# Second norm, transposes and router products of tiles 0 to 11 moved into the attention stage's last octet, with both stages in one block

## The chip, the cores and the metric

The kernel runs on one core of a Trainium2 chip. The metric is the device time of one execution in microseconds (us); lower is better. The engines are TensorE (PE, with its weight loads as PEld), VectorE (DVE), ScalarE (ACT), GpSimd (POOL) and SyncE (SP, which here only starts DMAs). Each engine runs its own instructions in their written order and waits on semaphores for the others.

## The reference, cut to what matters

Tokens are 2048 rows of 512 numbers (32 batches of 64). Two residual blocks are computed in float32:

```python
x = x + tanh(g_xattn) * xattn(layernorm(x), ctx, Wq, Wk, Wv, Wo)     # 32 heads of 128, 4 key/value heads
x = x + tanh(g_ffn)   * ffn(layernorm(x), router, experts, shared)
# ffn, for xt = layernorm(x):
scores = softmax(xt @ router_w + router_b) + router_bias             # 16 experts, 4 groups
# keep the best 2 groups, of these the best 2 experts; gate = their scores
y = sum over experts e of gate[:, e] * ((silu(xt @ w1 + b1) * (xt @ w2 + b2)) @ w3 + b3)
z = (silu(xt @ sw1 + sb1) * (xt @ sw2 + sb2)) @ sw3 + sb3            # shared expert, 256 wide
return y + z
```

## The kernel before, in words

The residual `y` stays on the chip as 16 tiles of 128 tokens by 512. Every float32 operand of a product is split into a rounded high part and the rest (`x_hi`, `x_lo`), and a product is three matmuls (`three_pass`, lines 84 to 86).

**Three stages, each in a block of its own.** Stage one makes keys, values and the transposed tokens. Stage two (`stage_two`) is attention: 128 steps m = 0 to 127, one for each of 4 key/value heads and 32 batches, grouped in octets of 8 steps; `octet(15, 3, NKV)` is the last octet, steps 120 to 127, and three more steps (128 to 130) let the pipeline run out. In step m PE computes the scores of batch m (L832, L834), turns the probabilities of batch m-1 (L872), projects queries for a later quad (only up to step 123), weighs the values of batch m-1 (`weigh`, into `ps_o`) and does half of an output projection (12 matmuls into `ps_y`). ACT copies the cross part of the scores (L672), makes `p_hi` (L678), the exponentials (L683) and `o_hi` (L691). DVE folds the scores (L758), takes the maximum (L760), makes `p_lo` (L763), adds an output pair to `y` (L738) or takes its statistics (L744), scales the probabilities (L779, `p_sb`) and makes `o_lo` (L783). In steps 120 to 127 DVE also aggregates one mean and variance a step (L749), and after step 130 the last eight together.

**Stage three** (`stage_three`) begins when all engines have left stage two. SP loads seven small tensors and the first half of the shared expert's weights; ACT loads the table for the square root and makes `std` of all 16 tiles; DVE takes the reciprocal. Then a front over 16 tiles: DVE normalises the even tiles and POOL the odd ones into a ring of 8 (`normed`); SP stores each to `xn_table`; PE transposes it into one of two banks (L1816); ACT makes `x_hi` (L1454) and DVE `x_lo` (L1585). After four tiles each, PE computes router products (`octet_logits`, L1793 and L1795, 8 matmuls), ACT copies them, and PE turns them (L1804). In between lie the splits of the shared weights and of `b3`. When the logits of all 16 tiles are turned, DVE starts the routing (L1625 and what follows): softmax, top-2, ranks, one-hot matrices (L1691 to L1696), slot tables (L1703 to L1709), while PE runs the shared expert's up products (`pe_up`, 24 matmuls an octet of tokens). Then come 31 slots of 256 rows each (gather, expert, scatter) and the end, which adds the experts' outputs and the second half of the shared expert to `y`.

Of the kernel before, what the change touches and what calls it, by code (L numbers as in the profile page):

```python
# [27 lines left out]
P = 128  # L28
# [64 lines left out]
def stage_one(nc, a, common, scratch):  # L93
# [4 lines left out]
    common["mean_var3"] = kept.enter_context(nc.sbuf_tensor("mean_var3", [P, TILES, 2], F32))  # L98
    scratch["k_full"] = nc.dram_tensor("k_full", (NKV, QUADS, P, QB * KEYS), F32, kind="Internal").ap()
    scratch["v_full"] = nc.dram_tensor("v_full", (NKV, QUADS, KEYS, QB, DH), F32, kind="Internal").ap()  # L100
    common["handed"] = handed = ExitStack()
    h = Buffers(nc, handed)
    w_raw = [h.sb(f"w_raw{i}", [P, 1024]) for i in range(2)]
    with ExitStack() as before:
# [3 lines left out]
    common.update(w_raw=w_raw, xt0=xt0, wq0=wq0, raw_in=[h.sem(f"raw_in{i}") for i in range(2)],  # L108
                  xt_in=[h.sem(f"xt_in{i}") for i in range(2)], w_hi_made=h.sem("w_hi_made"),
                  w_lo_made=h.sem("w_lo_made"))  # L110
# [369 lines left out]

def stage_two(nc, a, common, scratch):
    y, ident, gain = common["y"], common["ident"], common["gain_attn"]
    with ExitStack() as stack:  # L483
# [7 lines left out]
        kt = [b.sb(f"kt{i}", [P, 2, QB, KEYS], F32R) for i in range(2)]  # L491
        vt = [b.sb(f"vt{i}", [KEYS, QB, 2, DH], F32R) for i in range(2)]
        kt_raw = b.sb("kt_raw", [P, QB, KEYS])
        vt_raw = b.sb("vt_raw", [KEYS, QB, DH])
        q_hi = [b.sb(f"q_hi{i}", [P, QB, HG, SQ], F32R) for i in range(2)]
        q_lo = [b.sb(f"q_lo{i}", [P, QB, HG, SQ], F32R) for i in range(2)]
# [17 lines left out]
        kt_in = b.sem("kt_in")  # L514
        vt_in = b.sem("vt_in")
        k_hi_made = b.sem("k_hi_made")
        k_lo_made = b.sem("k_lo_made")
        v_hi_made = b.sem("v_hi_made")
        v_lo_made = b.sem("v_lo_made")
        stats_made = b.sem("stats3_made")  # L520
        w_hi_made, w_lo_made = common["w_hi_made"], common["w_lo_made"]
        queries = b.sem("queries")
        q_hi_made = b.sem("q_hi_made")
        q_lo_made = b.sem("q_lo_made")
        scored = b.sem("scored")
        cross_copied = b.sem("cross_copied")
        folded = b.sem("folded")
        max_made = b.sem("max_made")
        exp_made = b.sem("exp_made")
        rsums_made = b.sem("rsums_made")  # L530
        p_made = b.sem("p_made")
        p_turned = b.sem("p_turned")
        p_hi_made = b.sem("p_hi_made")
        p_lo_made = b.sem("p_lo_made")
        weighted = b.sem("weighted")
        o_hi_made = b.sem("o_hi_made")
        o_lo_made = b.sem("o_lo_made")
        halves = b.sem("halves")
        added = b.sem("added")
# [28 lines left out]
        block = stack.enter_context(nc.Block())  # L568

        @block.sync  # L570
        def _(sp):
# [59 lines left out]
        @block.scalar  # L631
        def _(act):
# [32 lines left out]
            def step(s, o, g):  # L665
# [32 lines left out]
                for i in splits_at(s.t, o, j):  # L698
                    split_piece(g, i)

# [10 lines left out]
        @block.vector  # L711
        def _(dve):
# [33 lines left out]
            def aggregate(tile):  # L746

                dve.wait_ge(stats_made, STEPS // 2 - TILES + tile + 1)
                dve.bn_aggr(mean_var[:, tile, :], stats[:, tile, :])  # L749

            def step(s, o, g):
# [19 lines left out]
                if isinstance(s.t, int) and s.t == STEPS // 8 - 1:  # L771
                    aggregate(j)
# [18 lines left out]
                for i in splits_at(s.t, o, j):  # L791
                    split_piece(g, i)

# [11 lines left out]
            for tile in range(8, TILES):  # L805
                aggregate(tile)

        @block.tensor
        def _(pe):
# [65 lines left out]
            def step(s, o, g):  # L875
# [7 lines left out]
                if s.query:  # L883
                    if p == 0:

                        pe.wait_ge(xt_in[quad_parity], 16 * (t + 1 + j // 4))
                    if last_octet and j >= 4:

                        pe.wait_ge(w_lo_made, PIECES * g + p + 1)

                    pe.wait_ge(q_lo_made, 4 * s.quad + p - 1)
                    project_queries(s.quad, quad_parity, p, 0)
                    project_queries(s.quad, quad_parity, p, 1)
                if s.pv:
                    weigh(s)
# [12 lines left out]
            for j in range(3):  # L908
                step(Step(16, j), 0, NKV)
    common["handed"].close()  # L910
# [12 lines left out]
class SharedHalf:  # L923
# [3 lines left out]
    def __init__(self, b, half, work, weights, ps_up, ps_down, y, moe):  # L927
# [7 lines left out]
        self.gate_copied = b.sem(f"s_gate_copied{half}")  # L935
# [18 lines left out]
    def act_silu(self, act, o):  # L954
# [3 lines left out]
        if o >= 2:  # L958
            act.wait_ge(self.h_made, o - 1)
        act.activation(self.silu[r][:], self.ps_up[2 * r][:], ACT.Silu,  # L960
                       bias=self.moe["shared_bias"][:, 0, self.half:self.half + 1]).then_inc(self.silu_made, 1)

    def act_gate(self, act, o):
        r = o % 2

        act.activation(self.h_sb[r][:], self.ps_up[2 * r + 1][:], ACT.Identity,
# [54 lines left out]
    def pe_up(self, pe, o, copied=False):  # L1021
# [10 lines left out]
        tokens = slice(512 * o, 512 * o + 512)  # L1032
        for k in range(2):
            for c in range(C):
                n = slice(INTER * c, INTER * c + INTER)
                last = three_pass(pe, self.ps_up[2 * r + k][:], self.w_hi[:, k, n], self.w_lo[:, k, n],
                                  self.moe["x_hi"][:, c, tokens], self.moe["x_lo"][:, c, tokens],
                                  c == 0, c == C - 1)
        last.then_inc(self.up_done, 1)
# [21 lines left out]
def stage_three(nc, a, common, scratch, out):  # L1061
# [7 lines left out]
    mean_var = common["mean_var3"]  # L1069
# [3 lines left out]
    RING = 8  # L1073
    CONSTS = 22
    WARM = 14
    with ExitStack() as stack:
        b = Buffers(nc, stack)
        x_hi = b.sb("x_hi", [P, C, T], F32R)
        x_lo = b.sb("x_lo", [P, C, T], F32R)
# [4 lines left out]
            "shared_bias": b.sb("shared_bias", [P, 2, 2]),  # L1084
# [8 lines left out]
                for name, dt in (("silu", F32), ("h_sb", F32), ("h_hi", F32R), ("h_lo", F32R))]  # L1093
        weights = [(b.sb(f"sw_hi{half}", [P, 3, 512], F32R), b.sb(f"sw_lo{half}", [P, 3, 512], F32R))
# [14 lines left out]
        with ExitStack() as early:  # L1109
            e = Buffers(nc, early)  # L1110
            normed = e.sb("normed3", [P, RING, D])

        with ExitStack() as middle:
# [29 lines left out]
            std = e.sb("std3", [P, TILES])  # L1143
            rstd = e.sb("rstd3", [P, TILES])
            eps = e.sb("eps3", [P, 1])
            rw_raw = e.sb("rw_raw", [P, C, E])
            rw = e.sb("rw", [P, C, 2, E], F32R)
            rb = e.sb("rb", [P, E])
            rbias = e.sb("rbias", [P, E])
            bias_rows = [e.sb(f"bias_rows{i}", [E, P]) for i in range(2)]  # L1150
            bias_rows_hi = [e.sb(f"bias_rows_hi{i}", [E, P], F32R) for i in range(2)]
            bias_rows_lo = [e.sb(f"bias_rows_lo{i}", [E, P], F32R) for i in range(2)]
            shared_rows = e.sb("shared_rows", [4, P])
# [14 lines left out]
            b3_raw = work[0][0][0:32]  # L1168
            logits_t = [work[1][i][0:2 * E] for i in range(2)]
            gates_t = [rows_in[1][0:2 * E, i] for i in range(2)]  # L1170
            fold = e.sb("fold", [2 * E, E])
# [10 lines left out]
        with ExitStack() as last:  # L1182
# [13 lines left out]
        ps_l = banks[2]  # L1196
        ps_turn = banks[3]
        ps_warm = banks[7]
        ps_rank = banks[4][:, 0:(TILES + 1) * E]
        ps_slots = banks[4][:, (TILES + 1) * E:(TILES + 1) * E + 2 * COLS]  # L1200
        ps_bias = banks[5]
# [3 lines left out]
        shared = [SharedHalf(b, half, work, weights[half], banks[0:4], [banks[6], banks[7], banks[4], banks[5]][:4 if half else 3], y, moe)  # L1205
                  for half in range(2)]
# [4 lines left out]
        std_made = b.sem("std3_made")  # L1211
        rstd_made = b.sem("rstd3_made")
        normed_even = b.sem("normed_even")
        normed_odd = b.sem("normed_odd")
        xn_stored = [b.sem(f"xn_stored{i}") for i in range(RING)]
        transposed = b.sem("transposed3")
        x_hi_made = b.sem("x_hi_made")
        x_lo_made = b.sem("x_lo_made")
        small_hi_made = b.sem("small_hi_made")
        small_lo_made = b.sem("small_lo_made")  # L1220
        b3_hi_made = b.sem("b3_hi_made")
        b3_lo_made = b.sem("b3_lo_made")
        logits_t_done = b.sem("logits_t_done")
        logits_t_copied = b.sem("logits_t_copied")
        logits_turned = b.sem("logits_turned")
        gates_copied = b.sem("gates_copied")
        bias_turned = b.sem("bias_turned")
        bias_copied = b.sem("bias_copied")
# [66 lines left out]
        def wait_normed(eng, n):  # L1295

            eng.wait_ge(normed_odd if n % 2 else normed_even, n // 2 + 1)

        def free_ring(eng, n):
            if n >= RING:  # L1300

                eng.wait_ge(transposed, n - RING + 1)
                eng.wait_ge(xn_stored[n % RING], 16)

# [3 lines left out]
        def _(sp):  # L1308
            for dst, src in small:
                sp.dma_start(dst, src).then_inc(small_in, 16)  # L1310
            shared[0].load(sp, a, sw_raw[0])
            for n in range(TILES):
                if n == 4:
                    sp.wait_ge(consts_made, 2)
                    sp.dma_start(b3_raw[0:E], a["L0_ffn_eb3"]).then_inc(b3_in, 16)
                    sp.dma_start(b3_raw[E:E + 1], line("L0_ffn_sb3")).then_inc(b3_in, 16)
                if n == 6:
                    shared[1].load(sp, a, sw_raw[1])
                wait_normed(sp, n)
                sp.dma_start(xn_v[n], normed[:, n % RING, :]).then_inc(xn_stored[n % RING], 16)  # L1320

# [28 lines left out]
        def _(pool):  # L1350
# [11 lines left out]
            def normalise(n):  # L1362
# [624 lines left out]
```

## Time and profile before

| | |
|---|---|
| median of 3 runs | 1589.07 us (1588.74 to 1591.45) |
| profiled execution, its own time | 1590.05 us |
| its span (first to last instruction) | 1588.3 us |
| mean granted TensorE clock | 0.98 |
| busy: PE, PEld, DVE | 94%, 83%, 62% of the span |
| busy: ACT, POOL | 49%, 11% of the span |

The busy shares are means over stages with different limits. Times inside the trace are us from the span's start. A timeline row holds start, duration, engine, line, operation, output and input tiles, sizes and count; in square brackets stands how long the engine was idle before it and who ended that.

### The profile page before, as it was taken

Reading aid. Unit: us, or ns where it says so; the run is one execution under the profiler, and the core shown is the slowest. Engines: PE = TensorE matmul, PEld = TensorE weight load, DVE = VectorE, ACT = ScalarE, POOL = GpSimd, SP = SyncE. Lnnn points to the kernel's source line nnn. Section 1 sums busy time; section 2 is a strip of 40 time slices with the busy share of each in tenths; the row PEclk is TensorE's granted clock in tenths of the full one; section 3 lists DMA queues with packets and bytes.
Section 4 is the critical chain, followed back from the end, with each engine's and each line's share of the span. In section 5 each row is a group of like instructions: output and inputs, shape, how many; then the busy total and the mean of one; then the engine's idle time right before and its main releaser. Section 6 shows DMA issues by size and latency. Waiting matters only on the chain. (4 is left out here: it accounts for less than half of the span.)

```text
span 1588.3 us, 26317 instructions
## 1 busy us (share of the span) xinstructions
PE 1489.7 (94%) x9150; PEld 1317.2 (83%) x9150; DVE 988.1 (62%) x1645; ACT 776.8 (49%) x2019; POOL 171.6 (11%) x169
## 2 busy tenths in 40 slices
PE   7999989999999999999999999999997788888886
PEld 5888878999999999899999899999995577877774
DVE  5322247666777666577666576766665587666648
ACT  3212236555656555466555465655553433766650
POOL 0000000000000000000000000000000512666640
PEclk9999999999999999999999999999999898999998
DMA  7575542211222121223111222211100404776437
GB/s 235 155 223 168 137 153 89 74 40 46 97 97 67 47 74 40 68 74 118 49 47 46 94 67 73 74 67 40 46 8 1 148 1 129 254 229 236 132 100 277
DMA packets 97447, 163.67 MB, mean 103 GB/s; under 512 B 12435, under 2 KB 47287, under 8 KB 93258
## 3 DMA queue, kind: packets, MB, share of 16 engines
q1 hardware_dynamic: 87370, 145.62, 28.2%
q0 software_dynamic: 9984, 16.82, 3.3%
q8 instruction: 58, 0.95, 0.2%
q14 instruction: 35, 0.29, 0.1%
HBM read 128.29 MB, written 49.81 MB: 112 GB/s over the span
## 5 line engine op out<-in xcount | busy, mean ns | idle before, releaser
L84 PE MATMUL ps_q<-xt,wq_hi 128*128 128x256 f32 x1024 | 302.5, 295 | 4.4 <-PEq L116 4.4
L85 PE MATMUL ps_q<-xt,wq_lo 128*128 128x256 f32 x1024 | 291.9, 285 | 0.0
L86 PE MATMUL ps_q<-xt,wq_hi 128*128 128x256 f32 x1024 | 291.9, 285 | 0.0
L683 ACT ACTIVATE s_sb<-s_sb,nmax 128x128 f32<-128x128 f32 x512 | 199.6, 391 | 130.3 <-DVE nmax L760 130.3
L758 DVE TENSOR_TENSOR s_sb<-ps_s,s_cross 128x512 f32<-128x512 f32 x128 | 88.5, 692 | 240.9 <-ACT s_cross L672 240.9
L672 ACT ACTIVATE s_cross<-ps_s 128x512 f32<-128x512 f32 x128 | 76.4, 597 | 277.6 <-PE ps_s L834 277.6
L84 PE MATMUL ps_y<-wo_hi,o_hi 128*128 128x512 f32 x512 | 203.0, 396 | 0.9 <-DVE y L738 0.9
L86 PE MATMUL ps_y<-wo_lo,o_hi 128*128 128x512 f32 x512 | 203.3, 397 | 0.0
L85 PE MATMUL ps_y<-wo_hi,o_lo 128*128 128x512 f32 x512 | 203.2, 397 | 0.0
L84 PEld LDWEIGHTS ps_q<-xt,wq_hi 128*128 128x128 f32 x1024 | 198.8, 194 | 5.0 <-issue 4.8
L85 PEld LDWEIGHTS ps_q<-xt,wq_lo 128*128 128x128 f32 x1024 | 199.0, 194 | 0.0
L86 PEld LDWEIGHTS ps_q<-xt,wq_hi 128*128 128x128 f32 x1024 | 198.5, 194 | 0.0
L832 PE MATMUL ps_s<-kt,q_hi 128*128 128x256 f32 x512 | 125.9, 323 | 9.4 <-issue 7.3
L1367 POOL MEMSET eps<- 128x1 f32 x1 | 0.1, 99 | 1233.8 <-POOLq L483 1233.8
L84 PEld LDWEIGHTS ps_y<-wo_hi,o_hi 128*128 128x128 f32 x512 | 96.6, 189 | 25.6 <-issue 2.6
L85 PEld LDWEIGHTS ps_y<-wo_hi,o_lo 128*128 128x128 f32 x512 | 97.1, 190 | 23.4
L86 PEld LDWEIGHTS ps_y<-wo_lo,o_hi 128*128 128x128 f32 x512 | 96.4, 188 | 22.7
L834 PE MATMUL ps_s<-kt,q_lo 128*128 128x128 f32 x512 | 115.0, 225 | 0.0
L832 PEld LDWEIGHTS ps_s<-kt,q_hi 128*128 128x128 f32 x512 | 97.2, 190 | 16.0 <-issue 8.2
L834 PEld LDWEIGHTS ps_s<-kt,q_lo 128*128 128x128 f32 x512 | 98.2, 192 | 5.3
L691 ACT ACTIVATE o_hi<-ps_o 128x512 fp32r<-128x512 f32 x128 | 76.9, 601 | 39.6 <-PE ps_o L86 39.5
L683 ACT ACTIVATION_READ_ACCUMULATOR s_sb<-s_sb,nmax 128x1 f32 x512 | 95.6, 187 | 0.0
(255 smaller groups left out, 3255.3 us busy)
## 6 DMA issues: line engine op xcount, KB each, us to landing
xt<-x_scratch SPq DMA_DIRECT2D x32, 1024.0 KB, 4.9
w_raw<-in_L_ffn_ew SPq DMA_DIRECT2D x93, 256.0 KB
v_full<-v_out SPq DMA_DIRECT2D x64, 128.0 KB, 2.5
k_full<-k_out SPq DMA_DIRECT2D x16, 512.0 KB, 2.8
w_raw<-in_L_xattn_Wq SPq DMA_DIRECT2D x16, 512.0 KB, 5.5
kt_raw<-k_full SPq DMA_DIRECT2D x32, 256.0 KB, 2.6
vt_raw<-v_full SPq DMA_DIRECT2D x32, 256.0 KB, 2.7
w_raw<-in_L_xattn_Wo SPq DMA_DIRECT2D x16, 512.0 KB, 3.9
```

What stands on the lines that cost most here:

```text
L84: pe.matmul(out, w_hi, x_hi, start=first, stop=False)
L85: pe.matmul(out, w_lo, x_hi, start=False, stop=False)
L86: return pe.matmul(out, w_hi, x_lo, start=False, stop=last)
L672: act.activation(s_cross[:], ps_s[:, :, 1], ACT.Copy).then_inc(cross_copied, 1)
L683: last = act.activation(s_sb[:, i], s_sb[:, i], ACT.Exp, bias=nmax[:, i:i + 1], accum_out=sums[:, i:i + 1])
L691: act.activation(o_hi[s.last_parity][:, :, s.last_token], ps_o[:], ACT.Copy).then_inc(o_hi_made, 1)
L758: dve.tensor_tensor(s_sb[:], ps_s[:, :, 0], s_cross[:], ALU.add).then_inc(folded, 1)
L832: pe.matmul(ps_s[:, i], q_hi[quad_parity][:, batch, heads].rearrange("p h t -> p (h t)"), k[:, :, batch], start=True, stop=False)
L834: last = pe.matmul(ps_s[:, i, 0], q_lo[quad_parity][:, batch, heads].rearrange("p h t -> p (h t)"), k[:, 0, batch], start=False, stop=True)
L1367: pool.memset(eps[:], EPS).then_inc(consts_made, 1)
```

## The change

Stage two no longer opens a block: its engine programs become functions (`sync`, `scalar`, `vector`, `tensor`), and stage three calls them first inside its own block. A new class `SecondNorm` holds the front. Tiles 0 to 11 are normalised on POOL, transposed over three banks (0, 1 and 7) and split inside steps 124 to 128; the router products of tiles 0 to 7 come in steps 128 and 129. Means, variances and inverse roots come in three rounds: tiles 0 to 8 at the end of step 120, tiles 9 to 11 at the end of step 125 (both with 15 small DVE instructions each, no ACT), tiles 12 to 15 with ACT's square root after the last step. Its table is loaded in step 128 by a one-element square root. The two weight splits of the first shared half lie in steps 125 (ACT) and 126 (DVE). The warm-up matmuls are gone. The load and split of the second shared half and the split of `b3` come later than before. The buffers of stage two are laid out in another order, the shared half's first up banks are 4 and 5, and its gate is copied by ACT in all four octets.

```diff
+class SecondNorm:
+    ROUNDS = ((0, 9), (9, 12), (12, TILES))
+    def tiles_in(self, s):
+        return {124: (0, 1), 125: (2, 3, 4), 126: (5, 6, 7), 127: (8, 9, 10), 128: (11,)}.get(s.m, ()) \
+            if isinstance(s.t, int) else ()
+    def inverse_root(self, dve, k):
+        lo, hi = self.ROUNDS[k]
+        v, r, w = self.std[:, lo:hi], self.root[:, lo:hi], self.trial[:, lo:hi]
+        # then(ins): ins raises the semaphore "rooted" and dve waits for it
+        then(dve.tensor_scalar(v, self.mean_var[:, lo:hi, 1], EPS, None, ALU.add))
+        then(dve.tensor_scalar(w.bitcast(whole), v.bitcast(whole), 1, None, ALU.logical_shift_right))
+        then(dve.tensor_scalar(r.bitcast(whole), w.bitcast(whole), -1.0, float(0x5f3759df), ALU.mult, ALU.add))
+        for i in range(3):
+            then(dve.tensor_tensor(w, r, r, ALU.mult))
+            then(dve.tensor_tensor(w, w, v, ALU.mult))
+            then(dve.tensor_scalar(w, w, -0.5, 1.5, ALU.mult, ALU.add))
+            out = self.rstd[:, lo:hi] if i == 2 else r
+            last = dve.tensor_tensor(out, r, w, ALU.mult)
...
+    def normalise(self, eng, n):
+        if n >= RING:
+            eng.wait_ge(self.transposed, n - RING + 1)
+            eng.wait_ge(self.xn_stored[n % RING], 16)
+        elif n == 2:
+            eng.wait_ge(self.signals["queries"], 128)
+            eng.wait_ge(self.signals["scored"], 124)
...
+    def turn(self, pe, n):
+        self.wait_normed(pe, n)
+        if n >= 3:
+            pe.wait_ge(self.x_lo_made, n - 2)
...
 def stage_two(nc, a, common, scratch):      # step of PE
+                for n in front.tiles_in(s):
+                    front.turn(pe, n)
+                if isinstance(s.t, int):
+                    common["pe_extra"](pe, m)
                 if s.pv:
                     weigh(s)
...                                          # step of DVE, after all else
+                for n in front.tiles_in(s):
+                    front.x_low(dve, n)
+                if isinstance(s.t, int) and m in (120, 125):
+                    lo, hi = front.ROUNDS[m // 125]
+                    for tile in range(lo, hi):
+                        last = aggregate(tile)
...
+                    front.inverse_root(dve, m // 125)
...                                          # stage three
+        def act_extra(act, m):
+            if m == 124:
+                act.activation(rw[:, :, 0], rw_raw[:], ACT.Copy).then_inc(small_hi_made, 1)
+            if m == 125:
+                shared[0].act_split(act, sw_raw[0])
+            if m == 128:
+                act.activation(spare[:], eps[:], ACT.Sqrt)
+            if m in (129, 130):
+                front.copy_logits(act, m - 129)
+        def dve_extra(dve, m):
+            if m == 124:
...
+            if m == 126:
+                shared[0].dve_split(dve, sw_raw[0])
+        def pe_extra(pe, m):
+            if m == 124:
...
+            if m in (128, 129):
+                front.logits(pe, m - 128, small_lo_made)
...                                          # PE after step 130
-            for i in range(WARM):
-                pe.matmul(ps_warm[:], ones_r[:], ...)
+            tensor_two(pe)
+            front.logits(pe, 2, small_lo_made)
+            pe.wait_ge(signals["added"], TILES * NKV)
+            for o in range(2):
+                front.turn_logits(pe, o)
+            for n in range(12, TILES):
+                front.turn(pe, n)
+            shared[0].pe_up_part(pe, 0, 0, 0, 2)
+            front.logits(pe, 3, small_lo_made)
+            front.turn_logits(pe, 2)
+            shared[0].pe_up_part(pe, 0, 0, 2, 3)
+            front.turn_logits(pe, 3)
+            shared[0].pe_up_part(pe, 0, 0, 3, C)
+            shared[0].pe_up_part(pe, 0, 1, 0, C)
...                                          # ACT after step 130
+            front.copy_logits(act, 2)
+            for n in range(12, TILES):
+                front.x_high(act, n)
+            front.copy_logits(act, 3)
             (high parts of the two bias rows)
+            for r in range(RING):
+                act.wait_ge(xn_stored[r], 32)
+            act.wait_ge(b3_in, 32)
+            act.activation(b3[0:32], b3_raw, ACT.Copy)
+            act.activation(b3[32:64], b3_raw, ACT.Copy).then_inc(small_hi_made, 1)
...                                          # DVE: after the one-hot matrices, before slot_token
             shared[0].dve_h_low(dve, 0)
+            shared[1].dve_split(dve, sw_raw[1])
```

## Rows read from the trace of the kernel before

**Rows 1.** Windows: length, busy us and count by engine, granted clock, DMA share, GB/s

```profile
1200.00:1220.00 20.00, 13.19 (x60) 10.59 (x61) 11.45 (x23) 9.35 (x33) 0.00 (x0) 0.91 0.00 0
1240.00:1260.00 20.00, 16.27 (x85) 11.82 (x84) 13.28 (x21) 9.57 (x17) 19.58 (x22) 0.89 0.78 266
```

**Rows 2.** Timeline of PE in the last octet: values weighed, output projection

```profile
1172.19 0.39 PE L84 MATMUL ps_o<-p_hi,vt 128*128 128x512 f32 x1
...
1211.13 0.50 PE L84 MATMUL ps_o<-p_hi,vt 128*128 128x512 f32 x1 [2.28 <-DVE p_lo L763]
...
1224.13 0.51 PE L84 MATMUL ps_o<-p_hi,vt 128*128 128x512 f32 x1 [1.41 <-DVE p_lo L763]
...
1228.86 0.47 PE L84 MATMUL ps_y<-wo_hi,o_hi 128*128 128x512 f32 x1 [0.94 <-DVE y L738]
...
1234.32 0.39 PE L86 MATMUL ps_y<-wo_lo,o_hi 128*128 128x512 f32 x1
```

**Rows 3.** Timeline of DVE in the last octet and behind it

```profile
1169.69 0.69 DVE L758 TENSOR_TENSOR s_sb<-ps_s,s_cross 128x512 f32<-128x512 f32 x1 [2.38 <-ACT s_cross L672]
...
1171.02 0.68 DVE L763 TENSOR_TENSOR p_lo<-ps_p,p_hi 128x512 fp32r<-128x512 f32 x1
...
1213.01 0.68 DVE L783 TENSOR_TENSOR o_lo<-ps_o,o_hi 128x512 fp32r<-128x512 f32 x1
1216.43 0.69 DVE L758 TENSOR_TENSOR s_sb<-ps_s,s_cross 128x512 f32<-128x512 f32 x1 [2.73 <-ACT s_cross L672]
...
1234.75 0.75 DVE L738 SCALAR_TENSOR_TENSOR y<-ps_y,gain_attn,y 128x512 f32<-128x512 f32 x1 [5.31 <-PE ps_y L86]
...
1236.14 0.62 DVE L749 BATCH_NORM_AGGREGATE mean_var<-stats 128x2 f32<-128x6 f32 x8
```

**Rows 4.** Timeline of ACT and DVE from the front's start to the routing

```profile
1237.04 1.28 ACT L1448 ACT_TABLE_LOAD   x1 [11.30 <-PEq L483]
1238.34 0.31 ACT L1448 ACTIVATE std<-mean_var,eps 128x16 f32<-128x16 f32 x1
...
1238.97 1.83 DVE L1579 TENSOR_SCALAR normed<-y,mean_var,rstd 128x512 f32<-128x512 f32 x3
...
1256.37 1.75 DVE L983 TENSOR_TENSOR sw_lo<-w_raw,sw_hi 128x1536 fp32r<-128x1536 f32 x1
...
1273.32 0.42 DVE L1625 TENSOR_TENSOR logits<-bank,rb 128x256 f32<-128x256 f32 x1 [1.80 <-PE bank L1804]
```

**Rows 5.** Timeline of PE in the front: turned logits, router products, transposes

```profile
1252.61 1.06 PE L1804 MATMUL bank<-fold,s_h_sb 32*128 32x16 f32 x8
...
1256.03 0.47 PE L1793 MATMUL bank<-x_hi,rw 128*32 128x512 f32 x1
...
1257.96 0.64 PE L1816 MATMUL bank<-ident,normed 128*128 128x128 f32 x4
```

**Rows 6.** Timeline of DVE in the routing: two small instructions in a row

```profile
1289.65 0.17 DVE L1671 TENSOR_SCALAR first_row<-first_slot 128x16 f32<-128x16 f32 x1
1289.85 0.42 DVE L1672 TENSOR_TENSOR masked<-bank,first_row 128x256 f32<-128x256 f32 x1
```

**Rows 7.** Timeline of POOL's normalising, and one DVE form beside POOL work and alone

```profile
1243.94 12.68 POOL L1364 TENSOR_SCALAR normed<-y,mean_var,rstd 128x512 f32<-128x512 f32 x6
...
1296.28 2.32 DVE L1691 TENSOR_TENSOR hot_row<-lanes,lane 128x1024 f32<-128x1024 f32 x1
...
1307.70 1.22 DVE L1691 TENSOR_TENSOR hot_row<-lanes,lane 128x1024 f32<-128x1024 f32 x1
```

**Rows 8.** DMA issues, 1100 to 1345 us: KB each, median us to landing

```profile
xn_table<-normed SPq DMA_DIRECT2D x16, 256.0 KB, 4.3
...
w_raw<-in_L_ffn_sw SPq DMA_DIRECT2D x6, 256.0 KB, 3.8
```

**Rows 9.** Timeline of DVE between the one-hot matrices and the slot tables

```profile
1312.22 0.69 DVE L996 TENSOR_TENSOR s_h_lo<-s_h_sb,s_h_hi 128x512 fp32r<-128x512 f32 x1
1314.80 0.22 DVE L1703 TENSOR_SCALAR later<-bank 128x62 f32<-128x62 f32 x1 [1.88 <-PE bank L1859]
```

More of the change, by code:

```diff
@@ L629, in _, with scalar @@
             over_octets(sp, octet)
-        @block.scalar
-        def _(act):
+        def scalar(act):
+            front = common["front"]
             def split_piece(g, i):
@@ L709, in _, with vector @@
                 step(Step(16, j), 0, NKV)
-        @block.vector
-        def _(dve):
+        def vector(dve):
+            front = common["front"]
             def split_piece(g, i):
@@ L804, in _, with tensor @@
             moments(TILES - 1, STEPS // 2)
[L805 to L809, printed above, removed]
+            for tile in range(12, TILES):
+                last = aggregate(tile)
+            last.then_inc(front.aggregated, 1)
+        def tensor(pe):
+            front = common["front"]
             def project_queries(quad, quad_parity, p, h):
@@ L923, with __init__ @@
 class SharedHalf:
-    def __init__(self, b, half, work, weights, ps_up, ps_down, y, moe):
+    def __init__(self, b, half, work, weights, ps_up, ps_down, y, moe, bias_copied):
+        self.bias_copied = bias_copied
         self.half, self.ps_up, self.ps_down, self.y, self.moe = half, ps_up, ps_down, y, moe
@@ L1167, in stage_three @@
             earlier_r = e.sb("earlier_r", [P, P], F32R)
-            b3_raw = work[0][0][0:32]
-            logits_t = [work[1][i][0:2 * E] for i in range(2)]
+            b3_raw = hot_row[0][0:32, 0:4].rearrange("p a b -> p (a b)")
             gates_t = [rows_in[1][0:2 * E, i] for i in range(2)]
-            fold = e.sb("fold", [2 * E, E])
+            logits_t = [w_raw[1][0:2 * E, i] for i in range(3)] + [gates_t[1]]
             probs = logits
@@ L1204, in stage_three @@
         ps_down = banks[4:8]
-        shared = [SharedHalf(b, half, work, weights[half], banks[0:4], [banks[6], banks[7], banks[4], banks[5]][:4 if half else 3], y, moe)
-                  for half in range(2)]
+        bias_copied = b.sem("bias_copied")
+        shared = [SharedHalf(b, 0, work, weights[0], [banks[i] for i in (4, 5, 0, 1)], [banks[i] for i in (6, 7, 4)],
+                             y, moe, bias_copied),
+                  SharedHalf(b, 1, work, weights[1], banks[0:4], [banks[i] for i in (6, 7, 4, 5)], y, moe, bias_copied)]
         small_in = b.sem("small_in")
```

452 lines of the change are left out of this document (239 added, 213 removed).

## Prediction

> **What bounds the kernel now.** I read the page first, for the shares of the engines; then the chain of work that ended last, for the stretches where it leaves PE; then windows of 20 us over the seam of stages two and three; last the timelines of each engine there. On the page PE is nearly always busy, so most of the kernel can't shrink by a reordering. The seam is different. Attention's last output product starts at 1234.32 us and its result is added from 1234.75 us [rows 2, 3]; routing can start only at 1273.32 us, when the last logits are turned [rows 4]. In these 38.6 us the work that must come after the last tile of `y` is small: the rest is twelve tiles whose `y` was complete before, plus a wait of every engine for the block to end. From 1273.32 us on the DVE chain of the routing sets the pace, since the chain of work goes from one routing instruction to the next up to the slot tables. So a change is worth what it moves the start of L1625. Call the end of the last output product E; before, E = 1234.7.
>
> Two more readings. In steps 124 to 127 PE is not the limit: it idles 2.28 us before it weighs, until DVE has made `p_lo` [rows 2]. DVE in turn idles 2.73 us between `o_lo` and the next fold [rows 3]. So a step has 2.3 us free on PE and 2.7 us on DVE; DVE work in excess of 2.73 us delays the next fold, `p_lo`, the weighing and so the whole step, one for one. In steps 120 to 123 PE also projects queries and has no gap: the weighing starts at 1172.19 us, while `p_lo` is done at 1171.70 us [rows 2, 3], a slack of 0.49 us.
>
> **What the moved work adds to attention (E moves by this).**
>
> Prices: x_low is a DVE instruction of the size of `o_lo`; these follow each other every 0.6 us, so three tiles cost 1.85 us. A small chained DVE instruction takes 0.17 us and the next starts after 0.20 [rows 6]; I take 0.21, so 15 of them cost 3.15. One aggregate is 0.62/8 = 0.08 [rows 3]. Four transposes take 0.64 and start to start about 0.5; eight router matmuls run from 1256.03 to 1257.96, 1.93 us [rows 5].
>
> - Step 120: nine aggregates 0.7, one wait and 15 small instructions 3.2, together 3.9, less one aggregate that went (0.1). DVE had 2.38 idle before the fold of step 121 [rows 3]; the excess is 1.4, and PE has 0.49 of slack: **+0.95**.
> - Step 124: two x_low 1.25, the router weights' low part and a copy 0.4, in all 1.65 under 2.73. POOL now normalises beside it, which can stretch an instruction with both inputs in the on-chip memory: `hot_row` took 2.32 us beside POOL work and 1.22 alone [rows 7]. `p_sb` is of that kind and half as long; from 0.2 to 1.1 more. I take **+0.2**.
> - Step 125: three x_low 1.85, three aggregates 0.25, 15 small 3.15, sum 5.25, excess 2.5; with 0.6 for a stretched `p_sb`, **+3.1**. ACT has the same three copies and the same split as DVE, but is busy 9.35 of 20 us where DVE is busy 11.45 [rows 1]; nothing taken.
> - Step 126: three x_low 1.85 and the split of 1.75 [rows 4] are 3.6, excess 0.9, with 0.6 for POOL **+1.5**.
> - Step 127: 1.85, nothing. Step 128: a tile's transposes and eight router matmuls, 2.4, in a gap of 1.41 [rows 2]: **+1.0**. Step 129: 1.93 in a gap of 0.94: **+1.0**.
> - PE's transposes of steps 124 to 127 (at most 1.6 us) lie in the 2.28 gap, nothing. If that gap were gone they would cost 5.5 us in all.
>
> POOL keeps up. Tiles 0 and 1 are ready after step 120. Steps 121 and 126 weigh at 1172.19 and 1211.13 us [rows 2], 7.8 us a step, so the last queries end near 1188.5 us with the delay; that frees tile 2, and at 12.68/6 = 2.11 us a tile [rows 7] tile 8 is done near 1203.5; tiles 5 to 7 are asked for near 1211. The root of tiles 9 to 11 comes near 1208 to 1212 us, when POOL is idle; POOL then needs 6.3 us, and PE asks for tiles 8 to 10 near 1220. SP sends the small loads as soon as its last value load is through, well before step 124. The shared weights go out behind the weighing of step 124 (1197 us) and land after 3.8 [rows 8], some 5 us before ACT splits them. The stores of tiles wait behind them on SP; ring place 2 is wanted back only at tile 10.
>
> Sum: 0.95 + 0.2 + 3.1 + 1.5 + 1.0 + 1.0 = 7.75, taken as 7.7 us, so E moves to 1242.4. Bounds: without any stretching by POOL 6.4, and 1.8 less if PE's clock no longer falls here (0.91 over 20 us [rows 1] is 1.8 us lost), 4.6. With 1.1 for POOL in three steps (1.9 more), 0.28 instead of 0.21 for each small instruction (30 of them, 2.1) and one more fall of the clock (1.8), 13.5.
>
> **What is left behind E.** Add 0.8, statistics 0.7, four aggregates 0.35: E+1.85. Square root 0.35 without the table load of 1.28 [rows 4], reciprocal 0.3, then 12, 13, 14 on DVE, 0.61 each (1.83/3): E+3.1, 3.7, 4.3; tile 15 on POOL E+4.8. PE meanwhile does the products of tiles 8 to 11 (1.9) and turns 8 logits (1.06 [rows 5]): E+3.0, then transposes; tile 15 waits for bank 0, freed by x_low of tile 12 at E+5.1, and ends at E+5.75. Six up matmuls 1.4, router products 1.9: E+9.05. ACT copies until E+9.7; turned at E+10.9. But DVE first makes the low part of `b3`: ACT gets there behind the bias rows (E+10.2), needs two copies (1.2) and DVE 0.7: E+12.1. The stores must have landed too: tile 15 goes out near E+5.2 and takes 4.3 [rows 8], just before E+10.2. I take **L1625 at E+12.1**, with 11 (no `b3` wait) to 15 (slow clock and a late store) as bounds.
>
> Behind L1625 nothing moves against it. PE has 9 of its 24 up matmuls done already, but waits for the mask anyway. The split of the second shared half (1.75) lies between 1312.9 us and the wait until 1314.80, an idle stretch of 1.88 us [rows 9]: hidden, and up to 1.7 if the PE clock is high there.
>
> **The sum.** Before 38.6; after 7.7 + 12.1 = 19.8; gain 18.8 us. Against the profiled execution, 1590.05 (span 1588.3 and 1.75 around it), this is 1571.3; the median lies 1.0 lower, so 1570.3 us.
>
> **A rule beside the trace.** The Trainium skill (SBUF — State Buffer, section SBUF: two separate sides) says that a GpSimd instruction holds the port pair for its whole length and that a VectorE instruction with two SBUF inputs fully blocks. The trace agrees in kind: `hot_row` lost 1.1 us beside POOL, short of a whole one of POOL's 2.11. By the rule at its hardest each `p_sb` in steps 124 to 126 waits 2.1, 5 us more than I took or 1575.
>
> **The rivals.**
> - *As forecast*, gain 15.5 to 21: chance 0.62.
> - *Attention pays more.* The small chained instructions cost 0.28 or more, POOL stretches three steps and the clock falls once more: E moves by 13 instead of 7.7, and the front takes 13.5: gain 12, time 1577. For it: no row shows such chains beside POOL. Against: POOL should be idle at both roots. Chance 0.19.
> - *It gains more.* The PE gap that the transposes fill was followed by a slow stretch [rows 1]; without it and without the `b3` wait the gain is 22 to 23, time 1567. Chance 0.12.
> - *The front was not what routing waits for*, or it is given back before the slots: no change, 1589. Against it: L1625 was released by the turned logits [rows 4]. Chance 0.02.
> - *Slower: POOL and DVE take turns.* If POOL's ten tiles inside steps 124 to 127 (21 us) were laid one by one in front of DVE's instructions, with its own gaps used up, E would move by 21 + 7.7 and the gain turn into a loss of 2, 1591. It decides from 18.8 us of such waits on. DVE instructions with a PSUM input show no stretching, and they are the most. Chance 0.05.
>
> **How the numbers follow.** A difference under 0.2% (3.2 us) can't be told from none. The range 1565 to 1579 takes in the bounds of both sums (gain 24 to 10) and leaves out the last two rivals and some of each tail. Faster 0.93, same 0.02, slower 0.05.
>
> **What would show it.** In the profile after: L1625 at 1254.5 us; the last output product ending near 1242.4; the fold of step 126 late by about 3 us behind the inverse root; PE's idle time before weighing partly filled with transposes; no table load between the last statistics and the square root; about 12 us from the last product to L1625, with DVE's low part of `b3` last. I am wrong if DVE's small instructions stand further apart than 0.25 us, if PE waits for a normalised tile in steps 125 to 127, if ACT waits for shared weights, or if the stores reach beyond E+10.

## The result, and the profile after

| | median, us | lowest to highest | runs |
|---|---|---|---|
| before | 1589.69 | 1588.74 to 1591.45 | 4 |
| changed | 1572.93 | 1566.85 to 1574.82 | 4 |

The changed kernel takes 0.9887 of the time before, with a 95% interval of 0.9858 to 0.9915: 16.8 us less. The forecast was 1570.3 with a range of 1565 to 1579, and faster with a chance of 0.93. The profiled execution took 1573.2 us with a span of 1571.4, so the two spans differ by 16.9 us.

The windows come first. They show each engine's busy time in five stretches: two at the end of attention, what is left behind it (1239.5 to 1252.7), and the routing in two parts.

```profile
core 0: us, PE busy (x) PEld busy (x) DVE busy (x) ACT busy (x) POOL busy (x), PEclk, DMA share, GB/s
1200.00:1220.00 20.00, 16.11 (x94) 13.90 (x93) 16.29 (x42) 11.47 (x31) 10.46 (x6) 0.91 0.45 159
1220.00:1239.50 19.50, 18.66 (x90) 13.83 (x89) 9.93 (x16) 8.48 (x21) 0.00 (x0) 1.00 0.01 1
1239.50:1252.70 13.20, 12.62 (x75) 8.86 (x73) 7.48 (x17) 5.78 (x12) 6.75 (x19) 1.00 0.22 82
1252.70:1272.70 20.00, 16.83 (x67) 13.83 (x68) 17.05 (x46) 6.39 (x9) 0.00 (x0) 0.83 0.13 40
1272.70:1296.00 23.30, 19.86 (x113) 17.64 (x112) 18.44 (x25) 8.72 (x16) 7.29 (x5) 0.86 0.00 1
```

The 38.6 us between the last product and the routing have shrunk to 13.0 us with PE almost always busy. In the 20 us behind it the granted clock is 0.83, where before the change it was 1.00 in the first 20 us of the routing: that is where the change gives something back.

The timeline of DVE in the last octet answers to [rows 3]: the end of step 120 with the first inverse root, one row of step 123, then steps 124 to 127.

```profile
1167.76 0.70 DVE L899 BATCH_NORM_AGGREGATE mean_var<-stats 128x2 f32<-128x6 f32 x9
1168.49 0.17 DVE L530 TENSOR_SCALAR std<-mean_var 128x9 f32<-128x9 f32 x1
...
1171.38 0.17 DVE L538 TENSOR_TENSOR rstd<-root,trial 128x9 f32<-128x9 f32 x1
1171.46 0.69 DVE L908 TENSOR_TENSOR s_sb<-ps_s,s_cross 128x512 f32<-128x512 f32 x1
...
1189.88 0.73 DVE L927 TENSOR_TENSOR p_sb<-s_sb,rsums 128x512 f32<-128x512 f32 x1
...
1197.58 0.69 DVE L927 TENSOR_TENSOR p_sb<-s_sb,rsums 128x512 f32<-128x512 f32 x1
...
1206.19 1.88 DVE L587 TENSOR_TENSOR x_lo<-bank,x_hi 128x512 fp32r<-128x512 f32 x3
1207.98 0.30 DVE L899 BATCH_NORM_AGGREGATE mean_var<-stats 128x2 f32<-128x6 f32 x3
1208.32 0.17 DVE L530 TENSOR_SCALAR std<-mean_var 128x3 f32<-128x3 f32 x1
...
1211.11 0.16 DVE L538 TENSOR_TENSOR rstd<-root,trial 128x3 f32<-128x3 f32 x1
1211.19 0.69 DVE L908 TENSOR_TENSOR s_sb<-ps_s,s_cross 128x512 f32<-128x512 f32 x1
...
1214.54 0.69 DVE L927 TENSOR_TENSOR p_sb<-s_sb,rsums 128x512 f32<-128x512 f32 x1
...
1217.54 1.75 DVE L1155 TENSOR_TENSOR sw_lo<-w_raw,sw_hi 128x1536 fp32r<-128x1536 f32 x1
1220.10 0.69 DVE L908 TENSOR_TENSOR s_sb<-ps_s,s_cross 128x512 f32<-128x512 f32 x1 [0.81 <-ACT s_cross L817]
```

Both folds behind an inverse root (L908 at 1171.46 and 1211.19) show no idle time: DVE itself is late. The 15 small instructions stand 0.206 us apart at the first root and 0.20 at the second. `p_sb` (L927) takes 0.73, 0.69 and 0.69 at the three places where POOL normalises beside it, and 0.69 elsewhere in the octet. POOL's rows for these tiles are these:

```profile
1189.31 14.96 POOL L561 TENSOR_SCALAR normed<-y,mean_var,rstd 128x512 f32<-128x512 f32 x7 [13.40 <-PE ps_q L86]
...
1211.47 6.19 POOL L561 TENSOR_SCALAR normed<-y,mean_var,rstd 128x512 f32<-128x512 f32 x3 [7.21 <-DVE rstd L538]
```

Of the seven in the first row, six take some 2.06 us, one after the other. The one that starts at 1197.55, 0.03 us before a `p_sb`, takes 2.60: where the two met, about half a microsecond was lost, and on POOL.

Behind the last product, DVE first, then PE, up to the one-hot products:

```profile
1239.75 0.75 DVE L888 SCALAR_TENSOR_TENSOR y<-ps_y,gain_attn,y 128x512 f32<-128x512 f32 x1 [5.99 <-PE ps_y L86]
...
1252.01 0.68 DVE L1768 TENSOR_TENSOR b<-hot_row,b 32x512 fp32r<-32x512 f32 x1 [0.88 <-ACT b L1653]
1252.73 0.42 DVE L1780 TENSOR_TENSOR logits<-bank,rb 128x256 f32<-128x256 f32 x1
...
1268.50 0.29 DVE L1821 TENSOR_TENSOR ties<-bank,thresholds 128x128 f32<-128x128 f32 x1 [1.14 <-PE bank L1970]
...
1285.20 2.07 DVE L1846 TENSOR_TENSOR hot_row<-lanes,lane 128x1024 f32<-128x1024 f32 x1 [4.21 <-PE bank L1991]
...
1297.14 0.22 DVE L1859 TENSOR_SCALAR later<-bank 128x62 f32<-128x62 f32 x1
...
1310.48 1.23 DVE L1892 TENSOR_TENSOR w_lo<-w_raw,w_hi 128x1024 fp32r<-128x1024 f32 x1 [0.25 <-ACT w_hi L1693]
```

```profile
1241.49 1.95 PE L613 MATMUL bank<-fold,w_raw 32*128 32x16 f32 x16
...
1249.73 1.06 PE L613 MATMUL bank<-fold,w_raw 32*128 32x16 f32 x8
...
1251.61 1.06 PE L613 MATMUL bank<-fold,rows_in 32*128 32x16 f32 x8
...
1265.11 0.39 PE L1968 MATMUL bank<-mask,earlier_r 128*128 128x272 f32 x1 [3.17 <-DVE mask L1812]
1265.34 3.06 PE L1970 MATMUL bank<-mask,ones_r 128*128 128x256 f32 x16
```

The last two rows stood like this before the change, with a shorter wait and shorter rank products:

```profile
1285.70 0.39 PE L1836 MATMUL bank<-mask,earlier_r 128*128 128x272 f32 x1 [1.01 <-DVE mask L1657]
1285.93 1.86 PE L1838 MATMUL bank<-mask,ones_r 128*128 128x256 f32 x16
```

The table load now stands at 1230.58 us, before the last statistics. Routing starts at 1252.73, 20.6 us earlier than in [rows 4]. At the slot tables (L1859 at 1297.14 against 1314.80 before [rows 9]) 17.7 are left, and 16.9 at the end.

| | before | forecast | after |
|---|---|---|---|
| last product ends (E) | 1234.7 | 1242.4 | 1239.7 |
| E to the first routing instruction | 38.6 | 12.1 | 13.0 |
| first routing instruction | 1273.3 | 1254.5 | 1252.7 |
| from there to the slot tables | 41.5 | 41.5 | 44.4 |
| slot tables to the end of the span | 273.5 | 273.5 | 274.3 |

### The profile page after: what moved, and what is told of

It is laid out like the page before. It is cut to its first block, busy times and chain, and to the rows that moved or that the text cites. A ratio compares the mean times of both kernels' runs of the same rounds, so it can differ in the third digit from the quotient of the medians.

```text
span 1571.4 us, 26321 instructions
## 1 busy us (share of the span) xinstructions
PE 1485.3 (95%) x9136; PEld 1316.6 (84%) x9136; DVE 987.5 (63%) x1670; ACT 777.0 (49%) x2022; POOL 180.7 (11%) x174
## 4 chain that ended last, share of the span: by engine, by line
PE 65%; issue 7%; DVE 6%; ACT 4%; DMA 2%; SPq 2%; another core or an unknown queue 1%; ACTq 0%; POOL 0%; POOLq 0%; DVEq 0%
PE ps_q L84 8%; PE ps_q L86 8%; PE ps_q L85 8%; PE ps_y L85 8%; PE ps_y L86 8%; PE ps_y L84 8%; PE ps_s L993 5%; PE ps_p L1033 3%; PE ps_o L84 2%; PE ps_s L995 2%; PE ps_o L86 2%; PE ps_o L85 2%; DMA w_raw<-in_L_ffn_ew 1%; ACT w_hi L1693 1%; DVE y L1934 1%
## 5 line engine op out<-in xcount | busy, mean ns | idle before, releaser
L908 DVE TENSOR_TENSOR s_sb<-ps_s,s_cross 128x512 f32<-128x512 f32 x128 | 88.5, 691 | 230.5 <-ACT s_cross L817 230.5
L561 POOL TENSOR_SCALAR normed<-y,mean_var,rstd 128x512 f32<-128x512 f32 x13 | 27.7, 2138 | 981.9 <-DVE rstd L538 966.6
```

What stands on the lines that cost most here:

```text
L561: eng.tensor_scalar(self.normed[n % RING][:], self.y[:, n, :], self.mean_var[:, n, 0:1], self.rstd[:, n:n + 1], ALU.subtract, ALU.mult).th ...
L908: dve.tensor_tensor(s_sb[:], ps_s[:, :, 0], s_cross[:], ALU.add).then_inc(folded, 1)
```

## The experiments

The experiments ran on two further chips, here the second and the third. Both run the kernels 14 to 15 us faster than the first one did; the kernel before takes 1575.81 us on the second (1572.73 to 1577.62, 11 runs) and 1574.65 on the third (1571.57 to 1578.26, 11 runs). Ratios are against these. For the changed kernel nearly all of that difference lies behind the slot tables: 260.3 us to the end of the span on the second chip, 274.3 on the first.

| kernel | chip | median, us (runs) | ratio, 95% interval |
|---|---|---|---|
| changed, unedited | second | 1558.54 (6) | 0.9886 (0.9867 to 0.9905) |
| root with one Newton round | second | 1556.41 (4) | 0.9876 (0.9860 to 0.9892) |
| idle matmuls before the mask | second | 1553.92 (4) | 0.9870 (0.9853 to 0.9888) |
| tiles 5 to 11 behind the block | second | 1563.53 (5) | 0.9920 (0.9906 to 0.9934) |
| one-hot products first | third | 1555.03 (6) | 0.9882 (0.9860 to 0.9904) |
| four edits together | third | 1550.27 (4) | 0.9847 (0.9833 to 0.9862) |
| the same, matmuls in step 126 too | third | 1551.25 (4) | 0.9849 (0.9834 to 0.9864) |
| two-input work on POOL | third | 1557.82 (1) | |

**1. The changed kernel again.**

> The changed kernel once more, unedited, as the base for the others of this set. Expected 1567 to 1575 us, ratio to before 0.989; in the trace the routing's first instruction at 1252 to 1253 us.

1558.54 us (1551.53 to 1561.01): below the 1567 to 1575 expected, as the chip is faster, with the ratio as expected. Its fold periods in steps 120 to 126 are those of the first chip within 0.02 us, and the slot tables follow the first routing instruction after 45.5 us (44.4 on the first chip). The pattern repeats; its runs spread over 9 us, which bounds what a difference of 2 us can say.

**2. Is it the small instructions that make steps 120 and 125 long?** The inverse root runs one Newton round in place of three, 7 small instructions in place of 15; the scales it gives are less exact.

```
-        for i in range(3):
+        for i in range(1):
```

> One Newton round instead of three in both inverse roots of tiles 0 to 11 (the normed rows are a little off; routing may differ for near ties). 16 small chained DVE instructions fewer, 8 in step 120 and 8 in step 125, 0.2 us each. Theory that DVE work in excess of its gap delays the step one for one: the last output product ends 2.2 to 2.6 us earlier (1.6 in step 125, 0.6 to 0.9 in step 120) and the time falls by 2 to 2.6 us. Rival, that the steps wait for something else (ACT's weight split, which ends just before step 126's copy, or PE): less than 0.8 us.

The steps from the fold of 120 to that of 127 take 7.68, 7.71, 7.68, 7.71, 7.36, 7.98 and 8.00 us; unedited 8.94, 7.40, 7.68, 7.68, 7.40, 9.55 and 8.91. From the fold of step 120 to the last addition (0.03 us behind E) it is 73.75 against 77.20: 3.45 less, where 2.2 to 2.6 was expected. Step 125 is 1.57 shorter, which is 8 times 0.20. Step 120 is 1.26 shorter and step 121 0.31 longer, together 0.95. And step 126, which the edit doesn't touch, is 0.91 shorter. The windows of both around it say why; first the unedited kernel on the same chip:

```profile
1202.00:1212.00 10.00, 6.61 (x40) 5.68 (x40) 8.95 (x30) 6.61 (x19) 2.78 (x2) 1.00 0.34 131
1212.00:1222.00 10.00, 9.16 (x44) 7.61 (x45) 8.14 (x13) 5.89 (x21) 4.31 (x3) 0.83 0.21 79
```

and with the short root:

```profile
1202.00:1212.00 10.00, 8.05 (x52) 6.93 (x51) 8.88 (x23) 7.19 (x18) 4.40 (x3) 1.00 0.52 199
1212.00:1222.00 10.00, 8.20 (x46) 6.94 (x47) 8.92 (x15) 6.78 (x24) 4.76 (x3) 1.00 0.21 79
```

PE waits 1.41 us in place of 2.99 before it weighs at the start of step 126, the granted clock stays at 1.00 behind it, and the step then takes 8.0 us. So the eight small instructions cost 2.5 us in the second root: 1.6 in its step and 0.9 through the clock in the next. In total time the edit is worth 2.1 us by medians, and the intervals overlap.

**3. Is the loss behind the first routing instruction the clock?** Twelve matmuls of 512 columns that nobody reads run before PE's wait for the mask.

```
+            for i in range(12):
+                pe.matmul(banks[7][:], ones_r[:], ones_r[:].unsqueeze(1).to_broadcast([P, 4, P]), ...)
             pe.wait_ge(mask_made, 1)
```

> Twelve idle matmuls (into a bank nobody reads) on PE while it waits for the routing's mask, where it now idles 3.17 us. Theory that the gain lost behind the routing's first instruction (20.6 us there, 17.7 at the slot tables) comes from PE running at 1.2 GHz after that gap: the rank matmuls take 1.9 instead of 3.06 us, DVE's wait for them goes, the up products of octet 2 keep 2.4 GHz, and DVE's wait for the first one-hot product falls from 4.2 to about 1 to 2 us; time 2 to 3 us less. Rival, that the loss is the second shared weight split put in front of the slot tables: no change beyond 0.5 us.

```profile
1259.34 2.90 PE L1966 MATMUL bank<-ones_r 128*128 128x512 f32 x12
1262.66 0.40 PE L1970 MATMUL bank<-mask,earlier_r 128*128 128x272 f32 x1 [0.42 <-DVE mask L1812]
1262.89 1.86 PE L1972 MATMUL bank<-mask,ones_r 128*128 128x256 f32 x16
```

The rank products take 1.86 us as before the change, in place of 3.42 (unedited, this chip). DVE waits no longer for `ties`, and before its third `hot_row` 1.08 us in place of 5.84. From the first routing instruction to the slot tables it is 41.15 us (1250.29 to 1291.44) against 45.50. Before the change this was 41.48 on the first chip, so what was given back there, 2.9 us, is all accounted for: PE has nothing to do for 3.2 us before the mask, its clock falls to 1.2 GHz, and the shared products between it and the one-hot matrices are late for DVE. The time falls by 4.6 us by medians, 0.9870 against 0.9886; the intervals overlap, so the time alone would not prove it.

**4. What is it worth to have tiles in the attention stage?** Only tiles 0 to 4 and the logits of 0 to 3 stay there; 5 to 11 go through the same three engines behind the block.

```
-        return {124: (0, 1), 125: (2, 3, 4), 126: (5, 6, 7), 127: (8, 9, 10), 128: (11,)}.get(s.m, ())
+        return {124: (0, 1), 125: (2, 3, 4)}.get(s.m, ())
```

> Tiles 5 to 11 are transposed and split, and the router products of tiles 4 to 7 made, behind the last output product instead of in steps 126 to 129; all else as in the changed kernel. Theory by rows: attention ends 2 to 2.5 us earlier (no x_low in step 126, no router products in 129), the tail gets 7 tiles of PE work at 0.53 and 1.9 of router products, 5.6 us; net 3 to 4 us slower than the changed kernel, 1575 to 1577. Rival, that a tile taken out of the tail is worth what it cost before (36 us for 16 tiles, 2.3 a tile): 14 to 16 us slower, near the kernel before.

From the fold of step 120 to the last addition it gets 0.6 us shorter (76.61), where 2 to 2.5 was expected. Two things are in it. Behind the fold of step 127 it is 1.2 less. But step 126 takes 9.47 us in place of 8.91 although its three `x_lo` are gone: without the transposes PE waits 4.44 us before it weighs, in place of 2.99, and the granted clock is 0.68 from 1212 to 1222 us, in place of 0.83. From the last addition to the first routing instruction it is 22.28 us. On the first chip it was 12.98 with a granted clock of 1.00, as here, and 13.85 in the unedited run on this chip with 0.88: longer by 9.3 at equal clock. PE's part of it, between E and the products of tiles 8 to 11:

```profile
1239.44 1.59 PE L574 MATMUL bank<-ident,normed 128*128 128x128 f32 x12
1243.09 1.31 PE L574 MATMUL bank<-ident,normed 128*128 128x128 f32 x8 [2.05 <-DVE x_lo L587]
...
1248.73 0.41 PE L599 MATMUL bank<-x_hi,rw 128*32 128x512 f32 x1 [1.53 <-DVE x_lo L587]
```

Three tiles are transposed, then PE waits 2.05 us for the `x_lo` that frees their bank, and later 1.53 for that of tile 11: 3.6 of the 9.3 us are this hand-over, the rest is work. The kernel is 5 us slower than unedited (0.9920 against 0.9886, intervals apart). Inside attention their work had cost 0.6 net, the clock counted in.

**5. Take DVE's wait for the bank away by order.** The one-hot products of octets 0 and 1 go before and between the shared up products in place of behind them.

```
-            shared[0].pe_up(pe, 3, True)
...
             for q in range(2, 4):   # (one-hot products of a quarter)
+                if q == 1: shared[0].pe_up_part(pe, 3, 0, 0, C)
+                if q == 2: shared[0].pe_up_part(pe, 3, 1, 0, C)
```

> PE takes the first one-hot products ahead of the up products of octet 3 and the last gate transposes, half of the up products between the first and second, the rest between the second and third; all else as in the changed kernel. Theory that DVE's wait of 4.2 us for the first one-hot product, and the low clock after PE's 3.44 us gap before the third, come from this order: DVE waits under 1 us, the slot tables come 4 to 6 us earlier behind the first routing instruction (44.4 us in the changed kernel), time 4 to 6 us less. Rival, that DVE's own chain with the second weight split behind it sets the tables: under 1 us.

Up to the first routing instruction this run has the times of the first chip within 0.1 us (1252.75 against 1252.73 there), so landmarks can be compared one by one. The slot tables come at 1293.89 against 1297.14, 3.25 us earlier. But the next thing is late instead, in PE's timeline:

```profile
1287.04 3.73 PE L1995 MATMUL bank<-hot_col,hot_row 128*128 128x124 f32 x32
1295.19 0.76 PE L84 MATMUL bank<-sw_hi,s_h_hi 128*128 128x512 f32 x1 [4.42 <-DVE slot_gate L1865]
1295.76 0.63 PE L85 MATMUL bank<-sw_hi,s_h_lo 128*128 128x512 f32 x1
```

PE now waits 4.42 us for the tables and does the following down products at 0.63 us each instead of 0.40. And DVE sets the tables itself: the one-hot products end at 1290.77, but the second weight split, which the change put in front of the tables, ends at 1293.98.

```profile
1292.23 1.75 DVE L1155 TENSOR_TENSOR sw_lo<-w_raw,sw_hi 128x1536 fp32r<-128x1536 f32 x1
```

So the rival of this expectation holds for what is left: in this order the split is no longer hidden. Slot 0's weights (L1892) come at 1309.20 against 1310.48. Of 3.25 us at the tables 1.3 are left 15 us later, and the ratio, 0.9882, can't be told from the unedited one; 4 to 6 us less was expected.

**6. Together.** Experiments 3 and 5, an inverse root of 12 small instructions that gives the same values up to rounding, and a tail in which the last four logits are turned in one go and the low part of `b3` is made behind the routing's first marks.

```
-                then(dve.tensor_tensor(w, r, r, ALU.mult))
+                then(dve.scalar_tensor_tensor(out=w, in0=r, scalar=-0.5, in1=r, op0=ALU.mult, op1=ALU.mult))
                 ...
-                then(dve.tensor_scalar(w, w, -0.5, 1.5, ALU.mult, ALU.add))
-                last = dve.tensor_tensor(out, r, w, ALU.mult)
+                last = dve.scalar_tensor_tensor(out=out, in0=w, scalar=1.5, in1=r, op0=ALU.add, op1=ALU.mult)
```

> Four edits on the changed kernel together: the idle matmuls before the mask, the one-hot products taken first, 12 instead of 15 chained instructions in each inverse root (same arithmetic, fused), and the last logits turned without up products between them, with the low part of b3 made while DVE waits for the exponentials. By rows: 0.6 in each root, 0.8 in the tail, 3 for the mask, 4 for the order, less 2 that the last two share: 7 to 8 us less than the changed kernel, ratio to before 0.983 to 0.985. Rival, that the gains are one and the same wait: 4 us.

1550.27 us (1550.03 to 1551.14): 0.9847 of the kernel before, 24.4 us less; its interval ends at 0.9862, that of the unedited change, taken on the other chip, begins at 0.9867. By these ratios the edits are worth 6 us, where 7 to 8 was expected. From the fold of step 120 to the last addition it is 75.97 us (77.2 before the edits), from the last addition to the first routing instruction 12.9 (13.9, at about the same granted clock), from there to the tables 40.9. It beats the kernel before and, across the two chips, the unedited change. What each of the four edits adds to the time was not taken apart, but the landmarks say that two of them don't add up. From the first routing instruction to the tables it is 41.15 us with the idle matmuls alone, 41.14 with the one-hot products first alone, and 40.87 with both: one and the same wait. And from there to slot 0's weights (L1892) it is 54.48 us in experiment 3 and 56.10 here, and the new order has brought PE's wait for the tables (4.35 us) with it. That this wait is the cause was not tested. Whether the idle matmuls without the new order would be faster still was not run.

**7. The clock in step 126 as well.** Nine more idle matmuls stand before the transposes of step 126.

> The same four and nine idle matmuls on PE in its 3 us gap of step 126. Theory that PE's low clock in step 126 is what makes this step 8.9 us, where DVE's work needs 8.2: 0.7 to 0.9 us less than the run of the four. Rival: DVE sets step 126 and nothing changes (within 0.3).

```profile
1205.78 2.32 PE L1057 MATMUL bank<-ones_r 128*128 128x512 f32 x9
1207.94 1.59 PE L573 MATMUL bank<-ident,normed 128*128 128x128 f32 x12
1209.86 0.50 PE L84 MATMUL ps_o<-p_hi,vt 128*128 128x512 f32 x1 [0.32 <-DVE p_lo L912]
```

PE's wait is 0.32 us (2.39 in experiment 6), the clock stays at 1.00, the step takes 8.01 instead of 8.91 (fold of step 120 to the last addition 75.06), as expected. Routing starts at 1247.41, 1.2 earlier than in experiment 6. The time shows nothing of it, 0.9849 against 0.9847, but intervals of 2.4 us to either side can't resolve 0.9. From the tables to the end of the span it is 263.2 us here and 259.2 in experiment 6, of the same instructions.

**8. POOL with two inputs.** Before it normalises each of tiles 3 to 6 POOL makes a product of two tiles in the on-chip memory (work of no use to the result).

```
+                if 3 <= n < 7:
+                    pool.tensor_tensor(front.normed[n][:], y[:, n, :], y[:, n, :], ALU.mult)
```

> POOL does one two-input instruction more (tile times itself, 128x512, into the ring place that it then overwrites) ahead of each of tiles 3 to 6, beside steps 123 to 125; the output is unchanged. In the changed kernel the p_sb instructions beside POOL's normalising took 0.69 us, as before. If a two-input POOL instruction blocks a DVE instruction with two inputs in the on-chip memory, p_sb of step 124 or 125 takes 1.2 to 1.8 us; if POOL's kind doesn't matter (rival: hot_row was slow for another reason), it stays at 0.69.

First POOL's timeline, then DVE's, where they meet:

```profile
1193.64 2.08 POOL L561 TENSOR_SCALAR normed<-y,mean_var,rstd 128x512 f32<-128x512 f32 x1
1195.68 1.44 POOL L1570 TENSOR_TENSOR normed<-y 128x512 f32<-128x512 f32 x1
1197.23 2.09 POOL L561 TENSOR_SCALAR normed<-y,mean_var,rstd 128x512 f32<-128x512 f32 x1
1199.28 1.04 POOL L1570 TENSOR_TENSOR normed<-y 128x512 f32<-128x512 f32 x1
1200.42 6.20 POOL L561 TENSOR_SCALAR normed<-y,mean_var,rstd 128x512 f32<-128x512 f32 x3
```

```profile
1195.53 0.69 DVE L927 TENSOR_TENSOR p_sb<-s_sb,rsums 128x512 f32<-128x512 f32 x1
1202.93 0.86 DVE L927 TENSOR_TENSOR p_sb<-s_sb,rsums 128x512 f32<-128x512 f32 x1
```

At 1195.5 both meet, DVE first by 0.15 us: `p_sb` keeps its 0.69, POOL's product takes 1.44 in place of 1.04. The next `p_sb` runs beside the one-input normalising and takes 0.17 more. Neither is what was expected (1.2 to 1.8 us, or 0.69 throughout). No `p_sb` happened to start inside a product of POOL, so whether that would make DVE wait is not settled by this run; what it shows is that the waiting can fall to POOL, as it did in the changed kernel at 1197.55.

## Why the prediction was right, and where it was off

- *Attention pays 7.7 us.* E came 5.0 later. Of this 0.5 lies ahead of the fold of step 120 (1162.00 and 1162.52), where none of the moved work stands; from there on it paid 4.5. Folds, before: 7.69, 7.70, 7.69, 7.70, 7.36, 8.93, 7.36 us apart in steps 120 to 126; after: 8.94, 7.38, 7.70, 7.70, 7.40, 9.55, 8.91. The term of step 120 (+0.95) is +0.93. The term of step 124 is +0.04 in place of +0.2. Step 125 was put at 3.1 and is 2.2 longer than an unslowed step; but before the change this step held a stretch of low clock (8.93 where its neighbours take 7.36), so against it only 0.6 is paid. The stretch has moved to step 126, which is 1.55 longer: 0.9 for the clock and 0.64 for DVE's excess, by the 8.00 of experiment 2. Forecast was 1.5, from 0.9 for DVE and 0.6 for POOL, so this term came out right by luck. Steps 128 and 129 pay 1.3 in place of 2.0. The mis-sized terms are thus POOL's, put at 1.4 and measured as next to none, the last two steps, and the clock: the sum took it as it was, the lower bound (4.6) as absent, and it was neither; it changed its place and its price (1.57 before, 0.9 after).
- *E to routing, 12.1.* It was 13.0. That the low part of `b3` would come last holds by a hair: it ends at 1252.69, PE's last turned logits at 1252.67, where the sum had 1.2 us between them. Mis-sized was turning: the row of 1.06 us with eight records [rows 5] is four matmuls of the kernel, two records each, and not eight. So the three rows after take 1.95, 1.06 and 1.06 where the sum had half: PE's last turn ends at E+13.0 in place of E+10.9. On the way over `b3` only the first of the three counts: the transposes start at E+3.7 in place of E+3.0, ACT's last copy of logits ends at E+10.7 in place of E+9.7, and `b3` follows as forecast.
- *Behind L1625 nothing moves against it.* This is the step that failed, by 2.9 us. The sum saw that PE had nine products less to do and waits for the mask anyway; it didn't ask what the longer wait (3.17 us in place of 1.01) does to PE's clock, nor that DVE waits for PE's bank later on. From the first routing instruction to the tables it took 44.4 us in place of 41.5, with a granted clock of 0.85 in place of 0.93. Experiment 3 gives the whole of it back.
- *The second shared split is hidden.* It is, just: DVE ends it at 1297.13, PE its one-hot products at 1297.10. Where PE is done earlier, as in experiment 5, it is not.
- *The rule on the shared port* (the Trainium skill, SBUF — State Buffer, section SBUF: two separate sides), by which a `p_sb` that starts inside an instruction of POOL would wait for its end. The trace disagrees for the one-input normalising: at most 0.04 us more in the changed kernel and 0.17 in experiment 8, far below POOL's 2.1. For the two-input `stacked` it doesn't disagree. The prediction set `hot_row`'s loss against 2.11, the length of another instruction; the `stacked` beside the `hot_row` of 1302.66 us in the trace before takes 1.26, of which 0.97 were left, and `hot_row` lost 0.84.
- *The rivals.* The 13 us more of attention did not come (5.0), POOL and DVE do not take turns, and routing did wait for what was moved: experiment 4, which moves seven tiles back, is 5 us slower.

So 18.8 forecast against 16.8 measured: 2.7 us better than forecast in attention, 0.9 worse behind it, 2.9 worse in the routing, and 0.8 in the slots. That the total came so near is in part luck: errors of 2.7 and 4.6 us had opposite signs. What the 0.8 in the slots is stays open. From the tables to the end of the span the eight profiled runs of the second and third chip take 258.0 to 263.2 us with the same instructions, so a single pair of profiles can't say.

## What to carry to other kernels

Work that fills gaps in a bound stage is nearly free if each gap is measured per engine, and the engine with the least slack sets the price; but list the low-clock stretches as terms of their own, with what PE did before each, since a change that shortens or lengthens a wait moves them. When a stage's front becomes shorter, look at the next wait of PE behind it: with less work left to do there it idles longer and may be slow for what follows. Gains at a landmark are not gains in time; follow each to the end of the span before adding it, and don't add two edits that take away the same wait.

## What the runs showed of the hardware

- Idle matmuls before a wait pay where DVE waits for PE next (4.35 us at the tables), while the 0.9 us by which they shorten step 126 can't be seen in the time.
- PE's wait of 3.01 us before weighing in step 126 was followed by a granted clock of 0.83 from 1212 to 1222 us, and the step took 8.91 us; with 2.39 (experiment 6) it took 8.91 too, with 4.44 (experiment 4) 9.47 at a granted clock of 0.68. With 1.41 and 0.32 us in its place (experiments 2 and 7) the clock stayed at 1.00 and the step took 8.0. The length of one pause doesn't decide alone: before the change the pauses of all four last steps were 2.3 us, and 0.83 followed in one of them (1200 to 1210 us).
- A one-input instruction of POOL hardly stretched a DVE instruction with two inputs in the on-chip memory (0.69 to 0.73 us; 0.86 once in experiment 8), and took 2.60 us itself in place of 2.08 where the DVE instruction started 0.03 us behind it, while DVE's `hot_row` beside POOL's two-input `stacked` took 2.06 to 2.32 us, and 1.22 alone.
- Eight profiled executions on the later chips differ by up to 5.2 us from the tables to the end, with the same instructions and a granted clock of 0.96 to 0.97 in that stretch.
